# An expert's output in two PSUM banks, gated and scattered in halves

## The reference

```python
scores = softmax(x @ router_w.T)                     # 4 x 1024 x 8
gate_vals, sel_idx = top_k(swap(scores), 257)        # per batch and expert
tokens = x[b_idx, sel_idx]                           # 257 rows of x
h = gelu(tokens @ w1 + b1)                           # 257 x 512
y = h @ w2 + b2                                      # 257 x 128
out = zeros_like(x).at[b_idx, sel_idx].add(y * gate_vals)
```

## Time and profile before

| | us |
|---|---|
| median of 3 runs | 2067.84 |
| the three runs | 2063.82, 2067.84, 2073.77 |
| the profiled execution | 2080.07 |
| its span, first to last instruction | 2078.3 |
| mean granted PE clock, as a share of full speed | 0.904 |
| expert layer, first pass | from about 753 to 1021 |
| expert layer, second pass | from about 1809 to the end |

### The profile page before, as it was taken

The page is one execution under the profiler, slowest core; times in us unless marked ns, Lnnn a source line. Parts: engine busy times, 40 slices in busy tenths (PEclk is TensorE's granted clock), DMA queues, the critical chain, the costliest instruction groups (busy, mean ns, idle before and its releaser), DMA issues. The chain is left out here.

```text
span 2078.3 us, 40685 instructions
## 1 busy us (share of the span) xinstructions
PE 1801.5 (87%) x15061; PEld 914.5 (44%) x15061; DVE 1406.0 (68%) x3124; ACT 1158.0 (56%) x2311; POOL 572.8 (28%) x812
## 2 busy tenths in 40 slices
PE   3779999999999978789468999999999999777895
PEld 1346666666655546466232222222233332245573
DVE  4556666666678645633359999999889998556531
ACT  1316666665565543222145888888888887332231
POOL 1021221221112235677440000001510000156674
PEclk9759999999999979888777999999999998578898
DMA  3764571751561015232230000000000000062324
GB/s 104 204 126 78 92 129 28 128 104 23 103 122 19 22 51 138 31 59 38 33 148 21 20 30 17 17 22 28 18 17 17 24 10 22 14 163 36 54 39 84
DMA packets 107958, 126.46 MB, mean 61 GB/s; under 512 B 14600, under 2 KB 69104, under 8 KB 107760
## 3 DMA queue, kind: packets, MB, share of 16 engines
q1 hardware_dynamic: 83568, 106.48, 22.0%
q0 software_dynamic: 24192, 17.38, 6.3%
HBM read 87.22 MB, written 35.65 MB: 59 GB/s over the span
## 5 line engine op out<-in xcount | busy, mean ns | idle before, releaser
L1100 DVE TENSOR_REDUCE mx<-wide 128x2 f32<-128x1024 f32 x512 | 604.7, 1221 | 55.5 <-PE wide L1010 43.4
L1134 ACT ACTIVATE pT<-bank 128x512 f32<-128x512 f32 x1024 | 556.6, 595 | 110.7 <-PE bank L1003 102.7
L797 ACT ACTIVATE pT<-bank 128x512 f32<-128x512 f32 (+3 forms) x768 | 351.4, 490 | 258.5 <-PE bank L653 239.6
L1003 PE MATMUL bank<-q_st,k_st 51*128 51x512 bf16 x1024 | 360.0, 397 | 20.1 <-ACT pT L1134 5.1
L1010 PE MATMUL wide<-k_st,q_st 48*128 48x512 bf16 x1024 | 352.8, 399 | 24.3 <-DVE mx L1100 13.9
L1019 PE MATMUL bank<-pT,vst 128*32 128x256 f32 x4096 | 340.2, 405 | 1.8 <-DVEq L1094 1.8
L765 DVE TENSOR_REDUCE mx<-wide 128x1 f32<-128x640 f32 (+3 forms) x256 | 257.6, 1022 | 101.9 <-PE wide L663 98.2
L663 PE MATMUL wide<-k_st,q_st 120*128 120x512 f32 (+3 forms) x768 | 314.3, 420 | 3.5 <-DVE mx L765 1.8
L653 PE MATMUL bank<-q_st,k_st 122*128 122x512 f32 (+3 forms) x768 | 301.5, 397 | 5.3 <-ACT pT L797 3.2
L1715 POOL DMA_INDIRECT acc_rows<-yg,idx x128 | 202.4, 1581 | 118.3 <-DVE yg L1974 85.4
L1003 PEld LDWEIGHTS bank<-q_st,k_st 51*128 51x128 bf16 x1024 | 90.3, 93 | 310.3 <-ACT pT L1134 267.0
(11 more groups left out here) (321 smaller groups left out, 1808.7 us busy)
## 6 DMA issues: line engine op xcount, KB each, us to landing
q_st<-rope_split SPq DMA_DIRECT2D x72, 256.0 KB
k_st<-rope_split SPq DMA_DIRECT2D x72, 256.0 KB
qk_split<-parts SPq DMA_DIRECT2D x8, 1024.0 KB, 8.3
q_st<-qk_split SPq DMA_DIRECT2D x96, 64.0 KB
k_st<-qk_split SPq DMA_DIRECT2D x96, 64.0 KB
qk_parts<-parts SPq DMA_DIRECT2D x8, 768.0 KB, 4.6
xn_rows<-xn SPq DMA_DIRECT2D x8, 512.0 KB, 3.5
w1b<-in_L_ffn_w SPq DMA_DIRECT2D x16, 256.0 KB
```

The source lines that it names most:

```text
L797: e.activation(pT[:, u % NPB, q0:HALF], bank[u % 2][:, q0:HALF], ACT.Exp, scale=scale).then_inc(s_p, 1)
L1003: e.matmul(bank[u % 2][:, :], k_st[at][64 * r:64 * r + KROW, jj, kc * P:(kc + 1) * P], q_st[at][64 * r:64 * r + KROW, jj, J * HALF:(J + 1) ...
L1100: e.tensor_reduce(mx[G % 2][:, kh, pair:GH:2, c], wide[w % 2][:, :].rearrange("p (r k) -> p r k", r=2), AX.X, ALU.max).then_inc(s_sf, 1)
L1134: e.activation(pT[:, u % NPB, :], bank[u % 2][:, :], ACT.Exp, scale=scale).then_inc(s_p, 1)
```

## The change

The second product's output is put in two banks. Groups 0 and 1 go to the first half of `bank[2]`, groups 2 and 3 to the first half of `misc`. Each half has its own increment of `s_y`, its own gating multiply (128 x 256 in place of 128 x 512), its own increment of `s_yev`, and the scatter of each batch waits for its half alone. PE waits for the bank of each half alone, by the multiply of the unit before. A half waits for the landed scatters of its own batch alone.

`facts_ps` gives up `misc` and moves to the last 32 columns of `bank[3]`, where the outputs of the 257th tokens lie. A bank must not be written and read at once, so three waits are new: the products of the 257th tokens (L1832 before) and the turning (L1754 before) wait until DVE has copied out the facts that were issued before them, and `read_slots(14)`, which runs in unit 12, waits until DVE has copied `ylT`.

```diff
-            facts_ps = misc[:, 0:NMH * 8].rearrange("p (m f) -> p m f", f=8)
-            y_ps = bank[2]
+            facts_ps = bank[3][:, HALF - NMH * 8:HALF].rearrange("p (m f) -> p m f", f=8)
+            y_ps = [ap.rearrange("p (m d) -> p m d", d=D) for ap in (bank[2][:, 0:2 * D], misc[:, 0:2 * D])]
+            reads_to = lambda n: min(n + 3, UNITS) - (1 if n in (NE - 2, NE - 1) else 0)
...
                     def scatter(n):
-                        e.wait_ge(s_yev, PRIME + n + 1)
                         for b in two:
+                            e.wait_ge(s_yev, PRIME + 2 * n + b + 1)
...
                     def read_slots(n):
+                        if n == LASTS[-1] + 3:
+                            e.wait_ge(s_ylT, PRIME + 2)
...
                     def turn_out(h):
-                        e.wait_ge(s_ylT, PRIME + 2)
+                        e.wait_ge(s_f, PRIME + reads_to(LASTS[-1] + 1))
...
-                        e.wait_ge(s_yev, PRIME + n)
                         for m in range(NMH):
+                            if m % 2 == 0:
+                                e.wait_ge(s_yev, PRIME + max(2 * n + m // 2 - 1, 0))
                             for k in range(KH):
-                                ins = e.matmul(y_ps[:, m * P:(m + 1) * P], hT[:, k, m * P:(m + 1) * P],
+                                ins = e.matmul(y_ps[m // 2][:, m % 2, :], hT[:, k, m * P:(m + 1) * P],
                                                w2b[:, ex, k, :], start=(k == 0), stop=(k == KH - 1))
+                            if m % 2:
+                                ins.then_inc(s_y, 1)
                             if m == 1:
                                 advance(other, n, 2)
-                        ins.then_inc(s_y, 1)
                         if n in LASTS:
                             e.wait_ge(s_a, PRIME + tiles_to(n) + KH + 1)
+                            e.wait_ge(s_f, PRIME + reads_to(n))
...
                             if k == 0:
-                                e.wait_ge(s_y, PRIME + n)
+                                e.wait_ge(s_y, PRIME + 2 * n)
...
-                        e.wait_ge(s_y, PRIME + n + 1)
-                        if n >= 2:
-                            for b in two:
+                        e.wait_ge(s_gk, PRIME + n + 1)
+                        for b in two:
+                            e.wait_ge(s_y, PRIME + 2 * n + b + 1)
+                            if n >= 2:
                                 e.wait_ge(s_sc[b], 32 * (n - 1))
-                        e.wait_ge(s_gk, PRIME + n + 1)
-                        e.tensor_tensor(yg[n % 2][:, :, :], y_ps[:, :].rearrange("p (m d) -> p m d", m=NMH),
-                                        gsl[n % 4][:, :, :].broadcast_to([P, NMH, D]), ALU.mult).then_inc(s_yev, 1)
+                            ms = slice(2 * b, 2 * b + 2)
+                            e.tensor_tensor(yg[n % 2][:, ms, :], y_ps[b], gsl[n % 4][:, ms, :].broadcast_to([P, 2, D]),
+                                            ALU.mult).then_inc(s_yev, 1)
```

## The result

| | median, us | lowest to highest | executions |
|---|---|---|---|
| before | 2067.84 | 2058.98 to 2073.98 | 9 |
| after | 2056.19 | 2050.12 to 2063.53 | 9 |

The ratio is 0.9943, with an interval from 0.9924 to 0.9961: 11.65 us less (2067.84 − 2056.19), where 6.3 were forecast. The profiled execution took 2058.62 us (span 2056.9). By the 0.5% of the prediction this is just "faster", a case that had 0.22; the time lies in the range.

What follows compares the result with a forecast made beforehand. Neither PE (87% busy) nor DVE (68%) was taken as saturated; waits for the gating multiply's start or end counted. −4.1 − 2.2 − 0.5 + 0.5 = −6.3 us gave 2061.5 us, range 2054 to about 2071.

Steps and rivals of the forecast that it cites:

- faster: Outcome case: the whole kernel gains more than 0.5%; chance 0.22.
- Tails: End of each expert layer: unit 15's first scatter starts 2.05 us sooner; −4.1 us over two layers.
- all that follows moves by 2.05 us as a piece: Layer end: everything behind unit 15's first scatter shifts earlier together, by 2.05 us.
- something else holds the scatter: Bound of the layer-end term: another wait, such as unit 14's first landing, holds unit 15's scatter; gain 0.
- Router: Bisection on DVE, nine places: multiply ends 0.27 us sooner, shortening PE's waits; −2.2 us.
- One sign: Halves running back to back in units where DVE had idled would show the forecast wrong.
- Unit 8: PE's wait for gathered rows: unit 6's first scatter starts 0.27 us sooner; −0.5 us over two layers.
- The sign that I gave: In unit 8, PE's wait for gathered rows would be 4.5 us in place of 4.80.
- New wait: Unit 12: PE's facts product waits for DVE's copy of bank 3, 0.25 us a layer; +0.5 us.
- Clock: Rival: PE's granted clock shifts, 1.7 us per group of sixteen matmuls; chance 0.16 to the good, 0.06 to the bad.
- clock to the good: Rival: three groups of sixteen matmuls gain PE's higher clock, 5.1 us; 2056.4 us, chance 0.16.
- The fixed cost of 32 more multiplies: Rival: on DVE, 0.16 us for each added multiply, +5.1 us; 2069.3 us with the tails, chance 0.06.

Runs made afterwards that it cites:

- Chip B: The chip of the second four of the twelve follow-up runs; the kernel before takes 2037.39 us on it.
- the output edit: Units 12 and 13 finish two groups of the first half's output rows each, not one a unit in 12 to 15; added to before: 0.9984.
- only unit 15 early: Changed kernel, but in units 0 to 14 the first half's multiply waits for the whole second product; 1.0058 to before, 2046.86 us.
- both halves late: Changed kernel, but every first half's multiply waits for the whole second product; 0.9989 and 1.0015 to before, on two chips.
- chip C: The chip of the last four of the twelve follow-up runs; the kernel before takes 2068.31 us on it.
- the fit: No kernel: 211 executions fitted with one clock slope, a level per chip and an offset per kernel; changed kernel −6.1 ± 1.1 us to before.
- chip A: The chip of the first four of the twelve follow-up runs; the kernel before takes 2072.52 us on it.
- facts in bank 3 only: Kernel before with only the slot facts moved to bank 3 and the three waits this needs; 1.0008 to before.
- the earlier output rows: Changed kernel with the first half's output rows finished two groups a unit in units 12 and 13; 0.9906 and 0.9912 to before, on two chips.

## Why the prediction was right, and where it was not

*Tails.* The step is right to 0.05 us: from the second product's start to the first scatter 2.84 or 2.85 us in all twelve layers of the six traces with an early unit 15, 4.84 or 4.85 in the ten of before and its variants. In the first layer it stays, 1.7 to 2.1 us. In the second it is worth nothing: the failed step is "all that follows moves by 2.05 us as a piece". The output writes did not belong to the piece. They hang on PE, and so they fell 2 us later against the scatters, where they delayed the last one. I had listed "something else holds the scatter" as a bound, but looked at what holds its start and not at what shares its DMA engines. The term is −2.0 + 0.4 = −1.6 us, not −4.1.

*Router.* Forecast −2.2 us. Chip B has hardly any pauses, so the places can be set side by side there. Before with the output edit, then the changed kernel with it, in unit 3, behind the multiply of unit 2 (timeline of PE, second layer):

```profile
1841.93 0.18 PE L1589 MATMUL bank<-count,same_row 128*128 128x3 bf16 x1 [0.95 <-DVE scan L1491]
```

```profile
1844.75 0.18 PE L1589 MATMUL bank<-count,same_row 128*128 128x3 bf16 x1 [0.69 <-DVE scan L1491]
```

The multiply's end comes 0.46 us after PE's last matmul in place of 0.73, and PE's waits behind it are 0.26 to 0.27 us shorter at eight of the nine places; at the ninth, unit 2 of the first layer, PE waits 1.31 us in both. Eight times 0.27 is the forecast. (In this pair PE's waits for DVE's scan sum to 13.6 and 11.6 us over both layers; the one for the normalised rows, unit 0 of the first layer, went from 0.84 to 0.58.) One sign was a poor one here: the halves of units 3 to 5 do run back to back, which was to show the forecast wrong, but the first starts 0.3 us ahead of PE's last matmul, in the time in which DVE used to idle, and that is enough. With the first half held back (only unit 15 early, same chip) the same waits are 0.12 us longer than in before, 1.07 us: that is what a second multiply costs where DVE has no idle time for the first. On the other chips PE's waits for DVE's scan in both layers sum to 16.4, 14.4 and 14.6 us in three traces of before, 12.5 and 16.3 with both halves late, 10.6, 10.6 and 11.2 in the changed kernel: 4.3 us less, but some of it comes back as issue time that nothing explains, as the 2.4 us in the rows above.

*Unit 8.* The scatter came 0.27 us sooner. From unit 6's second product to unit 8's turn the first pair of traces gives 21.90 and 22.03 us; the mean of the six layers of the changed kernel is 21.88, that of the ten of before and its variants 22.10. So 0.22 us a layer, −0.4 in all, where −0.5 was forecast. The sign that I gave, a wait of 4.5 us, was a poor one: it depends on when PE arrives.

*New wait.* 0.25 us a layer at the first product, as forecast, where DVE is in time. In three of six layers of the changed kernel's three traces PE waited 2.0 to 2.3 us, above my upper bound of 1.2 us for both layers. But the wait is not what cost them. In a trace of before on chip C, second layer, DVE's copy is late by the same remote wait, and PE does not wait for it (timeline, unit 12; PE's turn there began at 1989.98):

```profile
1991.54 0.28 PE L1742 MATMUL wide<-facts,picks 128*128 128x5 bf16 x5 [0.50 <-issue]
1992.32 0.49 DVE L1979 COPY ylT<-bank 128x128 f32<-128x128 f32 x2 [2.92 <-remote]
1993.04 0.60 ACT L1861 ACTIVATE xgT<-bank 128x512 f32<-128x512 f32 x1 [6.90 <-remote]
1993.69 2.07 PE L1801 MATMUL wide<-xgT,w1b 128*128 128x512 f32 x2 [0.47 <-ACT xgT L1861]
```

ScalarE's copy is late as well, PE's facts product comes in pieces, and the first product starts 3.71 us after the turn; in the changed kernel with its 2.32 us of waiting it is 3.81 us (1987.95 − 1984.14). So a stall that reaches all three engines lies under both, and with it the new wait makes a difference of 0.1 us. The term stays +0.5.

*Sum.* −1.6 − 2.2 − 0.4 + 0.5 is −3.7 us without stalls, against −6.1 ± 1.1 by the fit. PE's idle time in the two expert layers (their length less PE's busy time) lies between: 121.9, 121.1 and 119.4 us in before, 116.6, 117.9 and 113.4 in the changed kernel, 4.8 us less. The one to two and a half microseconds between are not assigned; the fit's clock and PE's idle time aren't separate things. For the pair with the output edit, where both ends gain (2.1 and 2.3 us) and there are no stalls, the same sum is −6.5 us and the fit gives −6.1 ± 2.1: there the terms account for the gain. That the forecast of −6.3 met the −6.1 of the plain pair so closely is luck: the tail was too large by 2.5, and what I can't assign is about as much. The chances were added up wrongly too: by the prediction's own list slower by more than 0.5% gets 0.03 and same 0.75, not 0.06 and 0.72.

*Clock.* Against it I argued that the gaps change by fractions of a microsecond. That failed in one place, and the clock moved the result as much as the work on chip A. Units 1 to 6 of the second layer (from ScalarE's copy of the gathered rows in unit 1 to that in unit 6) take 65.0 and 64.7 us in the changed kernel on the first chip and on A, 70.6 and 72.6 in before; on chip C 67.2 and 66.9. The other kernels without the early half take 67.7 (facts in bank 3 only) and 69.7 us (both late) on A, which lies between, and 68.5 on C (both late). The rows show where: PE's wait for gelu in the middle of unit 2's first product is 2.5 to 3.4 us in all six traces without the early half on these three chips, and 0.4 to 0.5 us in all four with it, in which PE's pauses fall into the facts product ahead of it instead. On chip B it is 1.62 us in all four traces, early half or not, the clock does not fall there, and the stretch takes 56.4 us with the early half in these units, 57.0 in before with the output edit and 58.8 with only unit 15 early. So the shorter wait goes with the early half and not with the split or bank 3, and only on chips with pauses; what links the two is not shown. The rival "clock to the good", three groups of 1.7 us, came true beside the forecast and not in its place: with it the time is 2056.4, and 2056.19 was measured, which is luck in its last digits.

*The fixed cost of 32 more multiplies* did not decide. The Trainium skill, "VectorE: DVE Perf Modes", section "The TRN2 errata — SBUF-src ops pay a fixed extra latency per instruction", advises against the smaller tile (it speaks of operands in SBUF; this multiply reads one from PSUM and one from SBUF). The fixed part is there (424 ns, 78 more than half of 692), but with both halves late and back to back the offset is +0.3 ± 1.1 us: DVE idles in front of most of them, and the first scatter starts 0.21 us sooner (4.63 us after unit 15's second product in place of 4.84).

*Open:* why only unit 15 early had so low a clock on chip B, and with it the worst ratio of all. At one clock it is +2.0 ± 2.1, in agreement with both halves late.

## What to carry to other kernels

When a step on the path starts earlier, list what else starts at that time by another chain: here the output writes, released by PE, slid onto the scatters that the change had pulled forward, and took the gain. Finishing those rows earlier freed it again. And in a kernel whose granted clock wanders, fit the time against the mean clock over all executions before a change of 0.5% is explained by its mechanism: between a quarter and a half of this gain was clock on the two chips where it could be told.

## What the runs showed of the hardware

The three chips differ by 35 us for the same kernel. One kernel (the earlier output rows) was traced on B and on C: of 29.5 us between the medians 29.0 lie in the expert layers (473.3 and 502.3 us), 9 of them more idle time of PE and 20 more busy time, at a granted clock of 0.87 and 0.88 on B and 0.84 on C. The idle time that B lacks is mostly pauses of PE named issue, which nothing in the profile explains, and there are waits of ScalarE and DVE named remote beside them. PE's waits in the second layer, of before on the first chip and of before with the output edit on chip B, where the facts product (`wide L1742`) has none:

```profile
PE bank L1789 <- issue: 4.8, 1, 4.8
PE wide L1742 <- issue: 4.2, 6, 1.1
```

```profile
PE bank L1789 <- issue: 4.9, 1, 4.9
```

In the expert layers PE has 8 to 20 such pauses a layer in each of the ten traces of A, C and the first chip, and 2 in each of the four of B; ScalarE's remote waits are 4 to 26 us a layer there and 0 on B. Many of them fall into the 32 short matmuls of the facts product. What they are no run shows. PE's idle time in the two layers is 100 to 105 us on B and 109 to 122 on the others.

The last indirect scatter took 3.3 to 3.5 us from issue to landing with nothing issued just ahead, 3.9 to 4.1 behind a load of 512 KB, and 6.4 to 6.6 behind that and 1 MB of writes. A load of activation tables took ScalarE 1.28 us. A multiply of f32 numbers from PSUM took DVE 292 ns for 128 columns, 424 for 256 and 692 for 512. Matmuls of 32 rows at different places of the array, into different banks, ran two at a time in 0.69 us, where two of one place and bank took 1.12.
